# A graph network on one core: where the steps of a tile's gated update stand in the groups of edge chunks

## The reference

```python
x = _layernorm(x + _L2_gnn_ref(x, edge_index, ...), axis=-1)

def _forward(x, edge_index, W, w_ih, w_hh, b_ih, b_hh, l0_w, l0_b, l1_w, l1_b):
    h = jnp.pad(x, ((0, 0), (0, s - x.shape[-1])))          # 6250 x 256
    def step(h, Wl):                                         # 5 rounds
        m = h @ Wl
        agg = jax.ops.segment_sum(m[src], dst, num_segments=n)
        gi = agg @ w_ih.T + b_ih
        gh = h @ w_hh.T + b_hh
        ir, iz, in_ = jnp.split(gi, 3, axis=-1)
        hr, hz, hn = jnp.split(gh, 3, axis=-1)
        r = jax.nn.sigmoid(ir + hr)
        z = jax.nn.sigmoid(iz + hz)
        ng = jnp.tanh(in_ + r * hn)
        h_new = (1.0 - z) * ng + z * h
        return (h_new, None)
    h, _ = jax.lax.scan(step, h, W)
    cat = jnp.concatenate([h, x], axis=-1)
    y = jax.nn.relu(cat @ l0_w.T + l0_b)
    y = jax.nn.relu(y @ l1_w.T + l1_b)
```

## Time and profile before

| | us |
|---|---|
| median of 3 runs | 11232.83 |
| the profiled execution, device time | 11230.72 |
| its span in the trace | 11229.0 |
| first gather of the gated rounds | at 4461.05 |
| last gather issued in the gated rounds | at 9953.1 |

### The profile page before, as it was taken

One profiled execution on the slowest core, in us unless ns is written; L12 is line 12 of the kernel. 1 busy time (PEld: TensorE's weight loads), 2 busy tenths in 40 slices (PEclk: granted clock), 3 DMA queues, 4 the chain that ended last, 5 costly groups with the idle time before them and its releaser, 6 DMA issues. The chain is left out here.

```text
span 11229.0 us, 162478 instructions
## 1 busy us (share of the span) xinstructions
PE 6373.5 (57%) x41938; PEld 5806.6 (52%) x41939; DVE 5443.9 (48%) x13456; ACT 2195.8 (20%) x7110; POOL 8085.3 (72%) x8298
## 2 busy tenths in 40 slices
PE   0000000045544444777777777777777788879996
PEld 0000000033333333777677767776777688868884
DVE  8885000044443443555455545554555456655554
ACT  0000000011113332111111111111111133335552
POOL 4777777777767776777677767776777677757773
PEclk9999999976665555888788878887888899989998
DMA  2000000022232223333433343334333433332222
GB/s 63 2 2 2 5 7 7 10 81 77 77 71 66 59 58 63 107 109 109 95 108 109 109 95 108 109 109 95 108 108 108 94 111 110 110 74 60 60 59 47
DMA packets 442833, 831.41 MB, mean 74 GB/s; under 512 B 179731, under 2 KB 260596, under 8 KB 442061
## 3 DMA queue, kind: packets, MB, share of 16 engines
q0 software_dynamic: 329728, 718.19, 25.7%
q1 hardware_dynamic: 112967, 111.54, 3.4%
HBM read 740.57 MB, written 88.61 MB: 74 GB/s over the span
## 5 line engine op out<-in xcount | busy, mean ns | idle before, releaser
L593 POOL DMA_INDIRECT rows<-state_table,idx x4160 | 4076.0, 980 | 1468.5 <-issue 1398.7
L639 DVE TENSOR_TENSOR agg<-agg,l_prod 128x250 f32 (+2 forms) x5824 | 2218.4, 381 | 3244.6 <-PE l_prod L616 1604.7
L616 PE MATMUL l_prod<-onehot,rows 128*128 128x125 f32 x16640 | 2573.8, 318 | 1066.7 <-DMA rows<-state_table,idx 506.3
L616 PEld LDWEIGHTS l_prod<-onehot,rows 128*128 128x128 f32 x16640 | 2399.3, 230 | 1190.9 <-DVE agg L639 933.4
L613 PE MATMUL l_prod<-rows,onehot 128*125 128x130 f32 (+1 forms) x3328 | 760.3, 403 | 2503.4 <-DMA rows<-in_x_dram,idx 1917.4
L613 PEld LDWEIGHTS l_prod<-rows,onehot 128*125 128x125 f32 x3328 | 664.8, 297 | 2578.0 <-issue 2179.5
L279 POOL DMA_INDIRECT slots_table<-rec_stage,row_stage x784 | 824.8, 1052 | 382.4 <-issue 242.3
L1507 POOL DMA_INDIRECT l_gathered<-xcol_table,l_idx x832 | 792.7, 953 | 314.1 <-issue 230.1
L593 POOL DMA_INDIRECT rows<-rel_table,idx x832 | 795.9, 957 | 299.4 <-issue 251.4
L622 DVE TENSOR_TENSOR onehot<-iota_row,rec 128x500 f32<-128x500 f32 x1465 | 986.9, 674 | 15.0 <-PEq L104 15.0
L593 POOL DMA_INDIRECT rows<-in_x_dram,idx x832 | 803.4, 966 | 254.2 <-issue 253.3
(11 more groups left out here) (274 smaller groups left out, 8691.9 us busy)
## 6 DMA issues: line engine op xcount, KB each, us to landing
rows<-state_table,idx POOLq DMA_INDIRECT x4160
slots_table<-rec_stage,row_stage POOLq DMA_INDIRECT x1568, 2.1
rel_table<-l_relrow SPq DMA_DIRECT2D x50, 500.0 KB
state_table<-l_row SPq DMA_DIRECT2D x200, 125.0 KB
rows<-in_x_dram,idx POOLq DMA_INDIRECT x832
rows<-rel_table,idx POOLq DMA_INDIRECT x832
l_gathered<-xcol_table,l_idx POOLq DMA_INDIRECT x832
slots_table<-fill SPq DMA_DIRECT2D x8, 936.0 KB
```

The source lines that it names most:

```text
L593: pool.indirect_dma_start(out=K["rows"][:, r, 0:width], out_offset=None, in_=table, in_offset=bass.IndirectOffsetOnAxis(ap=K["idx"][:, r:r ...
L616: last = pe.matmul(p[:, s * SLOT:s * SLOT + LANES], K["rows"][:, r, s * D:(s + 1) * D], oh, start=True, stop=True)
L639: dve.tensor_tensor(into, into, of, ALU.add).then_inc(S.added, 1)
```

## The change

The change touches the third layer alone. The places lag as before and no arithmetic is added or removed; what moves is the half of the group in which a step stands.

- In the rounds before the last, the products for r and h, with ACT's and DVE's part, go from n = 0 to n = 1, those for n and z from n = 1 to n = 2, and the new-state burst from n = 2 to n = 3. The transposes, ACT's copies and SP's row store go from n = 3 to n = 1 of the next group (`back`), there ahead of that group's products for r and h. DVE reads the tile's column number at n = 3, between the one-hot matrices and the burst, instead of at the group's start.
- In the last round `xt` and `hid` go into the next group (n = 0 and n = 1), `y` to n = 2 and the norm's scaling to n = 3 of it, and the transpose of x3 and `proj` into the group after that (`two`), at n = 1 and n = 2. ACT's square root goes from n = 0 to n = 3. The loops of the last round have one more turn written out at either end (`ahead=4, behind=2`).

The core of the diff:

```diff
-def turns(eng, rnd, body, rounds=1):
+def turns(eng, rnd, body, rounds=1, ahead=3, behind=1):
...
@@ gates of PE @@
-                if n == 0:
+                if n == 1:
                     if turn.first is not None and turn.place_in_round(b) == 0:
                         pe.wait_ge(comb_ok, rnd + 1)
 
                     pe.wait_ge(S.added, turn.chunk(b * GROUP) + CREDIT)
                     product(r_b, 0, [(w_comb, sums), (w_comb, sums), (w_hh, old), (w_hh, old)])
                     product(h_b, 2, [(w_hh, old), (w_hh, old)]).then_inc(rh_ps, 1)
-                if n == 1:
+                if n == 2:
                     product(n_b, 2, [(w_comb, sums), (w_comb, sums)])
...
@@ PE, rounds before the last @@
-                        now, _ = columns_of_places(nc, pe, PE, K, turn, b)
+                        now, back = columns_of_places(nc, pe, PE, K, turn, b)
                         for n in range(4):
                             if turn.chunks():
                                 sum_half(pe, K, S, prod, turn, 4 * b + n, STATE, False)
-                            if now is not None:
-                                gates(turn, n, b, now, rnd)
-                            if n == 3 and now is not None:
-                                pe.wait_ge(new_ok, turn.place(b) + 1)
+                            if n == 1 and back is not None:
+                                pe.wait_ge(new_ok, turn.place(b, 1) + 1)
                                 for s in range(2):
                                     last = pe.transpose(trs[0:LANES, s * D:(s + 1) * D], new[:, s, 0:LANES],
                                                         K["ident"][:])
                                 last.then_inc(rows_ps_ok, 1)
+                            if now is not None:
+                                gates(turn, n, b, now, rnd)
...
@@ ACT, rounds before the last @@
+                            if n == 1 and back is not None:
+                                act.wait_ge(rows_ps_ok, turn.place(b, 1) + 1)
+
+                                act.wait_ge(stored[b], (turn.pair - 2) * 16 + 16)
+                                act.copy(row[:, b, :], trs[0:LANES, 0:STATE]).then_inc(row_ok, 1)
+                                act.copy(state[:, :, nodes(back)], new[:, :, 0:LANES]).then_inc(kept, 1)
                             if now is not None:
                                 gate(turn, n, b, now)
...
@@ DVE, rounds before the last @@
-                    now, _ = columns_of_places(nc, dve, DVE, K, turn, b)
                     for n in range(4):
                         if turn.chunks():
                             add_half(nc, dve, K, S, prod, turn, 4 * b + n, into)
-                        if now is not None:
+                        if n == 3 and turn.has(b):
+                            now, = columns_of_places(nc, dve, DVE, K, turn, b, 1)
                             gate(turn, n, b, now)
+                        elif turn.has(b):
+                            gate(turn, n, b, None)
```

More of the change, by code:

```diff
@@ L1229, in last_body @@
                 for b in range(2):
-                    now, back = columns_of_places(nc, pe, PE, K, turn, b)
-                    odd = (b + 1) % 2
+                    now, back, two = columns_of_places(nc, pe, PE, K, turn, b, 3)
+                    one, other = (b + 1) % 2, b
                     for n in range(4):
@@ L1248, in last_body @@
-                        if n == 3 and back is not None:
-                            pe.wait_ge(x3t_ok, turn.place_in_round(b, 1) + 1)
+                            if turn.first is not None and turn.place_in_round(b, 1) == 0:
+                                pe.wait_ge(loaded, 16 * 5)
+                            if two is not None:
+                                pe.wait_ge(y_step, turn.place_in_round(b, 2) * 2 + 1)
+                            pe.wait_ge(xs_in[other], (turn.i - 2) * 16 + 16)
@@ new lines, in last_body @@
+                            pe.transpose(xt_ps[:, 0:LANES], xs[:, other, :], K["ident"][0:LANES, 0:LANES])\
+                                .then_inc(xt_ps_ok, 1)
+                        if n == 1 and two is not None:
+                            pe.wait_ge(x3_ok, turn.place_in_round(b, 2) + 1)
+                            if back is not None:
+                                pe.wait_ge(xt_ok, turn.place_in_round(b, 1) + 1)
+                            pe.transpose(x3t_ps[:, 0:LANES], x3[:, one, :], K["ident"][0:LANES, 0:LANES])\
+                                .then_inc(x3t_ps_ok, 1)
@@ L1250, in last_body @@
+                        if n == 2 and two is not None:
+                            pe.wait_ge(x3t_ok, turn.place_in_round(b, 2) + 1)
+                            if back is not None:
+                                pe.wait_ge(hid_ok, turn.place_in_round(b, 1) + 1)
                             v = x3t[:, 0:LANES]
@@ L1330, in last_body @@
                 for b in range(2):
-                    now, back = columns_of_places(nc, act, ACTE, K, turn, b)
-                    odd = (b + 1) % 2
+                    now, back, two = columns_of_places(nc, act, ACTE, K, turn, b, 3)
+                    one = (b + 1) % 2
                     for n in range(4):
@@ L1359, in last_body @@
                             last.then_inc(hid_ok, 1)
+                        if n == 2 and two is not None:
+                            act.wait_ge(proj_ps_ok, turn.place_in_round(b, 2) + 1)
+                            act.copy(K["agg"][0:LANES, bass.ds(two, D)], proj_ps[0:LANES, 0, :])
+                            if turn.has(b, 4):
+                                act.wait_ge(col_out[one], (turn.i + (b - 3)) * 16)
+                            act.copy(colrow[:, one, :], proj_ps[0:LANES, 1, :]).then_inc(proj_ok, 1)
+                        if now is not None:
+                            gate(turn, n, b, now)
+                        if n == 3 and back is not None:
+                            norm.deviation(act, K, turn.place_in_round(b, 1))
             stage_first(act, K, S, 0, LAST)
             combine(LAST)
-            turns(act, LAST, last_body, rounds)
+            turns(act, LAST, last_body, rounds, ahead=4, behind=2)
         @block.vector
```

167 lines of the change are left out of this document (68 added, 99 removed).

## The result

The changed kernel takes 11269.9 us (median of 8 runs, 11265.2 to 11271.9), the kernel before 11235.9 us in the same comparison: a ratio of 1.0029, 95% interval 1.0018 to 1.0040. The forecast was 11228 us with a range to 11262.

What follows compares the result with a forecast made beforehand. POOL was taken to bound the gated rounds, by standing still between rounds and by lengthened gathers. 6 + 9 - 20 = -5 us on 11230.7 gives 11225.7, the median 2.1 higher: 11228 us, range 11188 to 11262 (8 in 10).

Steps and rivals of the forecast that it cites:

- What bounds the kernel: Gated rounds: POOL sets the pace; only its standing still between rounds (150.7 us) and lengthened gathers (96 us) show.
- Inside the rounds: Within rounds: moved PE, ACT and SP work stays hidden behind POOL's gathers, set at zero.
- The four ends: Ends of rounds: transposes ahead of tile 49's products add, a faster last sum gives back; +6 us, 0 to 14.
- The end of the last round: Behind the last sum: later scaling, burst, products, square root and `proj` cost +9 us, between 5 and 13.
- POOL's own pace: Gathers beside DVE's update steps: shifted `u` and burst lengthen them less, -20 us, bounds -60 and +25.
- the rest follows at fixed distances: Within rounds: PE's sum starts when rows land, later steps keep fixed distances, so phases against gathers repeat between tiles.
- The saving: Gathers beside `u`: 0.3 us saved in about a third of the tiles, taken as 0.08 us a tile.
- The phase falls badly: Rival: burst or `u` lands on a gather's end in every group; 11323 us, at a third 11273; chance 0.15.
- Only the ends count: Rival: POOL's gathers keep their 980 ns and the ends cost 15 us, giving 11248 us; chance 0.17.
- the inferred remark of the Trainium skill: DVE against POOL: a `tensor_tensor` would not hold up descriptor generation, so moved DVE steps leave gathers as they are; 15 us.

Runs made afterwards that it cites:

- e4: Changed kernel with the row of numbers, sigmoid of z and tanh in PSUM in rounds 1 to 4: 11148.2 us, ratio 0.9923.
- e15: Kernel before with the row of numbers, sigmoid of z and tanh in PSUM in rounds 1 to 4: 11147.5 us, ratio 0.9924.
- e14: Changed kernel with the transposes and ACT's row copy of rounds 1 to 4 one half earlier: 11248.9 us, ratio 1.0014.
- e13: Kernel before with a small DVE memset of 128 columns ahead of each one-hot build of rounds 1 to 4: 11236.7 us, ratio 1.0002.

## Why the prediction was wrong, point by point

- **What bounds the kernel.** Right: POOL, in two ways, standing still between rounds and longer gathers. Waits for staged indices stayed at 0.3 us each.
- **Inside the rounds, nothing.** Right for PE, ACT and SP: with the gathers freed, e4 and e15 take the same time within 1 us.
- **The four ends, +6.** Measured +1.4. The timeline of the changed kernel at the end of round 1, answering to the earlier trace rows:

```profile
5552.16 2.04 PE L614 MATMUL l_prod<-onehot,rows 128*128 128x125 f32 x16 [1.36 <-DMA rows<-state_table,idx]
...
5554.42 2.06 DVE L637 TENSOR_TENSOR agg<-agg,l_prod 128x250 f32 x4 [2.52 <-PE l_prod L614]
...
5556.40 0.67 DVE L620 TENSOR_TENSOR onehot<-iota_row,rec 128x500 f32<-128x500 f32 x1
...
5556.99 0.41 DVE L1384 TENSOR_TENSOR l_dd<-state,l_ng 128x250 f32<-128x250 f32 x1
...
5558.36 0.79 PE L1210 MATMUL l_trs<-ident,l_new 128*125 128x128 f32 x2 [4.16 <-DVE l_new L1386]
...
5558.95 1.05 PE L1164 MATMUL l_rh<-agg,w_comb 128*128 x4
...
5566.47 0.37 ACT L1299 ACTIVATE l_gz<-l_nz,b_rz 128x125 f32<-128x125 f32 x1 [2.06 <-PE l_nz L1164]
...
5569.78 0.72 PE L1210 MATMUL l_trs<-ident,l_new 128*125 128x128 f32 x2 [3.35 <-DVE l_new L1386]
...
5575.04 0.95 POOL L591 DMA_INDIRECT rows<-state_table,idx  x1 [37.30 <-issue]
```

  The chain is as laid out: the last sum takes 2.04 us (3.77 before); builds, burst and transposes stand ahead of tile 49's products, which begin 4.53 us behind the first add instead of 2.19, 2.3 us added where 2.4 was forecast. Summed over the four ends, the way from the first add to tile 49's products is 9.4 us longer (9.6 forecast), the last sum and its way to the add 4.9 shorter (6 forecast), and the products to the sigmoid of z 1.3 longer (2.4 forecast; at this first end 7.5 us against 8.4, at the second 7.2 against 5.7). The term that was left out is the start of the last sum: it comes 1.0 us sooner behind the round's last gather on the mean (14.4 to 16.0 us against 15.5 to 16.7), 4.2 us in all. Why wasn't tested.
- **The end of the last round, +9.** Measured +7.4, inside 5 to 13.
- **POOL's own pace, -20 with -60 and +25 as bounds.** This is the step that failed: four rounds +36.4 and the last -8.7, so +28 where -20 was forecast, past the upper bound. Three things in it were wrong. The cause was read from the instruction that lay beside a long gather's later part (`u` at 5008.48) and not from the one under way at its start (the build of 5007.32, a row further up), and for the gather of 5016.66 the burst of 5017.02 was named in place of the build of 5016.43; `u`, with an input in PSUM, costs 0.003 us. The build was then left out, though there are four of it for one burst, and its losses are 59 of 89 us before. And "the rest follows at fixed distances" doesn't hold: in the trace of before the adds begin between 2.5 and 4.8 us behind a half's landing (8 halves in 10, by the landings' semaphores). The saving was worked out from the place of `u`, which had cost nothing, so there was nothing to save by moving it.
- **The rivals.** "The phase falls badly" has the direction and the kind of loss, longer gathers by a worse phase, at 0.11 us an update over 250 (36.4 us in 200 of them less 8.7 in 50). Its mechanism isn't what happened: it has the burst or `u` land on the end of a gather, while the loss is of builds under way at a gather's start, and the burst's part hardly moved (22.3 us before, 23.8 after). So it is luck that its 11273 us for a third of the full loss is 3 us from the measured time. It was given 0.15. "Only the ends count" is out, as the gathers did change; had they stayed, the measured ends would have given about 11242. What the prediction drew from the inferred remark of the Trainium skill, gathers as they are, is out. The rule on two SBUF inputs in the same section of the page "SBUF — State Buffer" would have named both the build and the burst, and cleared `u`.

## What to carry to other kernels

When a gather on POOL is longer than its neighbours, look at the DVE instruction that is under way at its start, not beside its end, and count the SBUF inputs: an instruction with two holds it up until it is through; of those with one, `u` and the adds cost nothing here, and a short `tensor_scalar` cost up to 0.10 us. Putting one operand of frequent two-input instructions in PSUM took more time out of this kernel (0.8% of the one before, 1.1% of the changed one) than any order of the update gave or cost; until that is done, a reordering elsewhere draws a new phase. In a kernel whose phase is better than chance the draw would be expected to lose more often than not; of three draws here the changed kernel and e14 lost and e13 came out even, too few to show it. An order of the update that is worth nothing on one chip was worth some 6% on chips where PE, ACT and DVE stood idle for nothing that the profile names, so a comparison on one kind says nothing on the other.

## What the runs showed of the hardware that I had not expected

- A gather's start is its sensitive point. A build that begins 0.08 to 0.6 us behind it costs nothing (443 cases before, 0.002 us each); one that began ahead of it costs its own rest less 0.12 us, up to 0.51 us. With another instruction right ahead of the build (e13) the full cost reaches builds that begin up to 0.09 us behind the start.
- The one-hot build with one input in PSUM is as long as with both in SBUF (671 and 674 ns for 500 columns), so the remedy costs DVE nothing.
- Between chips the same program differed by a third (11233 against 14828 to 15029 us), with DVE's build of the same length on both.
